# Message stage: turning a channel's factors to tokens in 64-row tiles, as products with a 64x64 identity

## The chip, the cores and the metric

The kernel runs on 1 core of one Trainium2 chip. The metric is the device time in microseconds of one execution. The times of this text are the medians of several executions.

## The reference, cut to what matters

The program is a small transformer: an attention layer, a mixture-of-experts layer, a "message" layer, and the experts layer once more, each added to x (4 batches of 1024 tokens of 128 features). The change lies in the message layer, which for each batch and each of C = 16 channels of rank R = 64 computes:

```
qz_u = qz @ ternary_factor_u.T * SCALE          # (batch, tokens, C*R)
qz_v = qz @ ternary_factor_v.T * SCALE
message_F = einsum('bcsr,bctr->bcst', qz_u, qz_v)
qh = sigmoid(message_F)
qh_v1 = einsum('bcst,bctr->bcsr', qh, qz_v)
qh_v2 = einsum('bcst,bcsr->bctr', qh, qz_u)
message_G = (qh_v1 @ ternary_factor_u + qh_v2 @ ternary_factor_v) * SCALE
```

All of it is float32.

## The kernel before

The phases follow one another: set-up, attention, experts, message, experts. `message_phase` works through 4 x 16 = 64 channels, one after the other, in a software pipeline. For one channel the factors of all 1024 tokens lie in `uv32`, a tile of 128 rows and 1024 columns: rows 0 to 63 are the sources' factors (u), rows 64 to 127 the targets' (v), the columns are tokens. `own` and `swap` hold them again, split in a high and a low part, the second with its halves of rows exchanged by DMA.

TensorE (PE) has these blocks for a channel. All of them are written out by hand in one order, in `body(b, c, n, p)`, so the order of work on PE is that of the code:

- `factors`: six products into the two PSUM banks `unit0` and `unit1`; ACT copies them to `uv32` and `own` (`empty_factors`), POOL makes the low part.
- `by_token`: `uv32` turned so that tokens are the rows. It takes eight 128x128 tiles of `uv32`, and writes four turned tiles to `unit0` and four to `unit1`. ACT copies each bank to `tok` (`empty_tokens`).
- `forces`, four times (j = 0 to 3): twelve products of 64 rows, in pairs on rows 0 to 63 and 64 to 127 of the array, into the banks `f_ps0` and `f_ps1`; ACT takes the sigmoid (`sigmoids`).
- `onto_targets`, four times: four float32 products with 64 columns of `tok` as weights.
- `onto_sources`, twice: sixteen such products with `sigT`, the sigmoid turned by DVE and shuffled by DMA.
- `message`: four float32 products of 64 rows into `unit0` and `unit1`, which DVE adds up in `msgT`.

In the loop, `by_token(n + 1)` stands between `onto_sources(n - 1, 1, ...)` and `forces(n, 3, p)`. It waits until ACT has taken the factors out of the unit banks (`uv_taken`). Behind it on PE stand `forces(n, 3)`, `onto_targets(n, 2)`, and then `message(n - 1)`, which waits until both banks were copied to `tok` (`tok_taken`), because it writes the same banks.

On ACT the order of a channel is `sigmoids` 0 and 1, `empty_factors`, `sigmoids` 2, `empty_tokens`, `sigmoids` 3.

Of the kernel before, what the change touches and what calls it, by code (L numbers as in the profile page):

```python
# [14 lines left out]
P = 128  # L15
BATCH, SEQ, DIM = 4, 1024, 128
TILES = SEQ // P
# [10 lines left out]
CH, RANK = 16, 64  # L28
# [1536 lines left out]
def message_phase(nc, k):  # L1565

    PAIRS = TILES // 2
    SIDE = TILES // 2
    MOVES = 16
    CHANNELS = BATCH * CH  # L1570
    with ExitStack() as ctx, ExitStack() as phase:
        def sb(n, shape, dt=F32):
            return ctx.enter_context(nc.sbuf_tensor(f"m_{n}", shape, dt))
# [3 lines left out]
        def sem(n):  # L1577
            sems.append(ctx.enter_context(nc.semaphore(f"m_{n}")))
            return sems[-1]

        def ps(n, width):
            return ctx.enter_context(nc.psum_tensor(f"m_{n}", [P, width], F32))
# [6 lines left out]
        uv32 = sb("uv32", [P, SEQ])  # L1589

        own, swapped_uv_st = ([sb(f"{n}{i}", [P, 2, SEQ], F32R) for i in range(2)] for n in ("own", "swap"))
        (own_hi, own_lo), (swap_hi, swap_lo) = ([[t[:, a, :] for t in both] for a in range(2)] for both in (own, swapped_uv_st))
        tok = [sb(f"tok{i}", [P, TILES, 2, RANK]) for i in range(2)]
        sig = [[sb(f"sig{i}{s}", [P, SEQ]) for s in range(2)] for i in range(2)]

        turned = [sb(f"turned{g}", [P, 4, 4, 8, STACK]) for g in range(2)]
# [6 lines left out]
        v2_ps, v1_ps = ps("v2_ps", HALF), ps("v1_ps", HALF)  # L1603
        unit = [ps(f"unit{i}", HALF) for i in range(2)]
# [3 lines left out]
        w_high, w_ready, uv_full, uv_taken, lo_ready, tok_full, tok_taken = (  # L1608
            sem(n) for n in ("w_high", "w_ready", "uv_full", "uv_taken", "lo_ready", "tok_full", "tok_taken"))
# [9 lines left out]
        def permuted(tile, h):  # L1619

            return tile.rearrange("p (s q a) -> p q s a", s=TILES, a=STACK)[:, 2 * h:2 * h + 2, :, :]

        def natural(tile):
            return tile.rearrange("p (q s a) -> p q s a", q=2, a=STACK)

        def tile_of(tile, st):
            return tile[:, st * P:(st + 1) * P]

        def channels(eng, body):

            for b in range(BATCH):
                for c in range(2):
                    body(b, c, b * CH + c, c)
                with eng.Fori(1, CH // 2 - 1) as cc:
                    for p in range(2):
                        body(b, 2 * cc + p, b * CH + 2 * cc + p, p)
                for c in (CH - 2, CH - 1):
                    body(b, c, b * CH + c, c % 2)

        def first(n):  # L1640
            return isinstance(n, int) and n == 0

        def final(n):
            return isinstance(n, int) and n == CHANNELS - 1

        def at(c, number):
            return isinstance(c, int) and c == number

        @block.sync
        def _(sp):  # L1650
            for to, of in ((slice(0, RANK), slice(RANK, P)), (slice(RANK, P), slice(0, RANK))):
                sp.dma_start(swapped_uv[to, :], k["uv"][of, :]).then_inc(factors_swapped, 16)

            def swap(m, p):

                sp.wait_ge(lo_ready, m + 1)
                dst, src = swapped_uv_st[p], own[p]
                sp.dma_start(dst[0:RANK, :, :].bitcast(F32), src[RANK:P, :, :].bitcast(F32)).then_inc(swapped[p], 16)
                sp.dma_start(dst[RANK:P, :, HALF:SEQ].bitcast(F32), src[0:RANK, :, HALF:SEQ].bitcast(F32)).then_inc(swapped[p], 16)

            def shuffle(n, g, groups):
                for i in groups:
                    for j in range(4):
                        sp.dma_start(sigT[g][j * STACK:(j + 1) * STACK, i, :, :, :],
                                     turned[g][i * STACK:(i + 1) * STACK, j, :, :, :]).then_inc(shuffled[g], 16)

            swap(0, 0)

            def body(b, c, n, p):
                sp.wait_ge(turn_ready, 8 * n + 4)  # L1670
                shuffle(n, 0, range(2))
                if not final(n):
                    swap(n + 1, 1 - p)
                shuffle(n, 0, range(2, 4))
                sp.wait_ge(turn_ready, 8 * n + 8)
                shuffle(n, 1, range(4))
            channels(sp, body)

        @block.tensor
        def _(pe):  # L1680
# [26 lines left out]
            def by_token(m):  # L1707

                pe.wait_ge(uv_taken, 2 * m + 2)
                for i in range(2):  # L1710
                    for t in range(4):
                        mm = pe.transpose(unit[i][:, t * P:(t + 1) * P], tile_of(uv32[:, :], 4 * i + t), k["ident"][:, :])  # L1712
                    mm.then_inc(tok_full, 1)

            def forces(n, j, p):

# [14 lines left out]
            def onto_targets(n, j, p):  # L1731

                if j == 0:
                    pe.wait_ge(tok_taken, 2 * n + 2)
                    if not first(n):

                        pe.wait_ge(v2_taken, n)
                pe.wait_ge(sig_ready, 8 * n + 2 * j + 2)
                for s in range(2):
                    for h in range(2):  # L1740
                        mm = pe.matmul(v2_ps[h * RANK:(h + 1) * RANK, :], tok[p][:, j + s * SIDE, 0, :],  # L1741
                                       sig[j % 2][s][:, h * HALF:(h + 1) * HALF], start=(j == 0 and s == 0), stop=(j == PAIRS - 1 and s == 1))
                mm.then_inc(p2_done, 1)

            def onto_sources(n, g, p):

                pe.wait_ge(shuffled[g], 256 * n + 256)
                if not (first(n) and g == 0):

                    pe.wait_ge(v1_taken, 2 * n + g)  # L1750
                for jj in range(TILES):
                    for h in range(2):
                        mm = pe.matmul(v1_ps[h * RANK:(h + 1) * RANK, g * 2 * P:(g + 1) * 2 * P], tok[p][:, jj, 1, :],  # L1753
                                       sigT[g][:, :, 2 * h:2 * h + 2, jj, :].rearrange("p i s a -> p s i a"), start=(jj == 0), stop=(jj == TILES - 1))
                mm.then_inc(p1_done, 1)

# [26 lines left out]
            turn_z(0)  # L1783
            factors(0, 0, 0, 0)
            by_token(0)

            def body(b, c, n, p):
# [29 lines left out]
            for g in range(2):  # L1817
                onto_sources(CHANNELS - 1, g, 1)
# [3 lines left out]
        @block.scalar  # L1822
        def _(act):
            act.wait_ge(var_ready, 1)
            act.activation(dev[:, :], spread[:, :], ACT.Sqrt).then_inc(dev_ready, 1)

            def high_z(b):
                for i in range(2):
                    act.wait_ge(z_full, 2 * b + i + 1)
                    act.copy(permuted(zT_hi[:, :], i), natural(unit[i][:, :])).then_inc(zT_high, 1)  # L1830

            def empty_factors(m, p):

                if not first(m):

                    act.wait_ge(lo_ready, m)
                for i in range(2):
                    cols = slice(i * HALF, (i + 1) * HALF)
                    act.wait_ge(uv_full, 2 * m + i + 1)
                    act.copy(uv32[:, cols], unit[i][:, :])  # L1840
                    act.copy(own_hi[p][:, cols], unit[i][:, :]).then_inc(uv_taken, 1)  # L1841

            def empty_tokens(m, p):
                for i in range(2):
                    act.wait_ge(tok_full, 2 * m + i + 1)
                    act.copy(tok[p][:, 4 * i:4 * i + 4, :, :].rearrange("p t a r -> p (t a r)"), unit[i][:, :]).then_inc(tok_taken, 1)  # L1846

            def sigmoids(n, j):

                act.wait_ge(f_full, 4 * n + j + 1)  # L1850
                if not (first(n) and j < 2):

                    act.wait_ge(p2_done, 4 * n + j - 1)
                    act.wait_ge(turn_ready, 8 * n + 2 * j - 2)
                for s in range(2):
                    act.activation(sig[j % 2][s][:, :], f_ps[s][:, :], ACT.Sigmoid).then_inc(sig_ready, 1)  # L1856

            high_z(0)
            empty_factors(0, 0)
            empty_tokens(0, 0)  # L1860

            def body(b, c, n, p):
                sigmoids(n, 0)
                sigmoids(n, 1)
                if not final(n):
                    empty_factors(n + 1, 1 - p)
                sigmoids(n, 2)
                if not final(n):
                    empty_tokens(n + 1, 1 - p)
                sigmoids(n, 3)  # L1870
                if at(c, CH - 2) and b + 1 < BATCH:
                    high_z(b + 1)
            channels(act, body)
# [200 lines left out]
```

## Time and profile before

| | |
|---|---|
| time, median of 3 executions (lowest, highest) | 3334.19 us (3330.05, 3337.33) |
| the profiled execution: time, span | 3331.9 us, 3330.1 us |
| mean granted TensorE clock | 0.937 of full speed |
| PE matmul, PE weight load, DVE, ACT, POOL busy, share of the span | 87%, 54%, 53%, 43%, 22% |

The profile is one execution of the program on the chip. PE stands for TensorE's matmuls, PEld for its weight loads, which overlap them. A matmul's duration in it is its latency through the array, and matmuls are pipelined; so what a stream of them costs is read from the distance between their starts. The granted clock is 1.00 at 2.4 GHz and 0.50 at 1.2 GHz. The message phase runs from about 1272 us to about 2912 us of the span.

### The profile page before, as it was taken

The numbers are of one execution on the slowest core, as the hardware profiler recorded it, in microseconds if no ns is written. First come the engines' busy times: TensorE is split into PE (matmuls) and PEld (weight loads), VectorE is DVE, ScalarE is ACT, GpSimd is POOL, SyncE is SP. The second block draws the span as 40 slices with busy tenths as digits, with TensorE's granted clock in tenths as the row PEclk, the third lists the DMA queues.
The fourth block names the chain that finished last, engine by engine and source line by source line (L and its number), as shares of the span: only waits on it lengthen the run. The fifth ranks groups of instructions, "written<-read, shape, count | busy, mean of one in ns | idle before, by whom it ended". The sixth has DMA issues, their size and how long they took to land. (4 is left out here: it accounts for less than half of the span.)

```text
span 3330.1 us, 55832 instructions
## 1 busy us (share of the span) xinstructions
PE 2907.6 (87%) x18642; PEld 1797.9 (54%) x18643; DVE 1755.1 (53%) x3207; ACT 1416.6 (43%) x2072; POOL 721.6 (22%) x866
## 2 busy tenths in 40 slices
PE   2888888889548996999999999999999999945897
PEld 1555554555437873555555555555555555444786
DVE  3656555554445664544554555555455555445565
ACT  1454554545424443444444444444444444332443
POOL 4131220311436330111111111111111111062632
PEclk7899999999759997999999999999999999966998
DMA  9000000000212215888888888888888888731122
GB/s 164 14 12 9 14 13 8 13 14 7 86 32 60 82 44 138 200 195 201 200 185 201 201 195 195 196 200 195 201 193 195 199 201 200 174 96 32 57 69 78
DMA packets 205987, 397.16 MB, mean 119 GB/s; under 512 B 45586, under 2 KB 118171, under 8 KB 201627
## 3 DMA queue, kind: packets, MB, share of 16 engines
q1 hardware_dynamic: 196634, 376.35, 49.1%
q0 software_dynamic: 9216, 19.02, 1.7%
q8 instruction: 82, 1.34, 0.2%
q14 instruction: 55, 0.44, 0.0%
HBM read 35.23 MB, written 31.75 MB: 20 GB/s over the span
## 5 line engine op out<-in xcount | busy, mean ns | idle before, releaser
L1943 DVE STREAM_TRANSPOSE m_turned<-m_sig 128x1024 f32<-128x1024 f32 x512 | 613.2, 1226 | 595.0 <-ACT m_sig L1856 575.3
L1856 ACT ACTIVATE m_sig<-m_f_ps 128x1024 f32<-128x1024 f32 x512 | 496.4, 1022 | 607.1 <-PE m_f_ps L1728 607.1
L1741 PE MATMUL m_v_ps<-m_sig,m_tok 128*64 128x512 f32 x2048 | 496.0, 605 | 0.0
L775 DVE TENSOR_REDUCE a_maxima<-a_pair 128x2 f32<-128x1024 f32 (+3 forms) x384 | 351.6, 953 | 272.3 <-PE a_pair L449 210.3
L1753 PE MATMUL m_v_ps<-m_sigT,m_tok 128*64 128x256 f32 x4096 | 465.5, 380 | 7.2 <-DMA m_sigT<-m_turned 7.2
L1728 PE MATMUL m_f_ps<-m_swap,m_own 64*128 64x512 f32 x1536 | 442.8, 421 | 11.0 <-DMA m_swap<-m_own 8.8
L1728 PE MATMUL m_f_ps<-m_own,m_swap 64*128 64x512 f32 x1536 | 442.9, 421 | 0.0
L593 ACT ACTIVATE a_prob<-a_pair 128x1024 f32<-128x1024 f32 (+3 forms) x384 | 303.9, 819 | 282.8 <-PE a_pair L461 282.4
L1753 PEld LDWEIGHTS m_v_ps<-m_sigT,m_tok 128*64 128x64 f32 x4096 | 293.7, 137 | 212.2 <-issue 69.5
L1728 PEld LDWEIGHTS m_f_ps<-m_swap,m_own 64*128 64x128 f32 x1536 | 270.4, 186 | 141.8 <-issue 86.2
L1880 POOL TENSOR_TENSOR m_own<-m_uv,m_own 128x1024 fp32r<-128x1024 f32 x64 | 152.0, 2375 | 840.5 <-ACT m_own L1841 840.5
L446 PE MATMUL a_pair<-k_apart,a_qT 128*128 128x512 f32 (+3 forms) x768 | 228.1, 392 | 69.6 <-DVE a_maxima L775 36.6
L1728 PEld LDWEIGHTS m_f_ps<-m_own,m_swap 64*128 64x128 f32 x1536 | 270.3, 186 | 3.4
L461 PE MATMUL a_pair<-a_qmT,k_apart 128*128 128x512 f32 (+3 forms) x768 | 238.5, 404 | 21.9 <-ACT a_prob L593 7.3
L1741 PEld LDWEIGHTS m_v_ps<-m_sig,m_tok 128*64 128x64 f32 x2048 | 124.1, 136 | 239.1 <-issue 239.1
L1329 POOL DMA_INDIRECT back_rows<-f_y_rows,f_goes_to x160 | 155.1, 970 | 263.8 <-DVE f_y_rows L1505 256.4
L446 PEld LDWEIGHTS a_pair<-k_apart,a_qT 128*128 128x128 f32 x768 | 137.6, 207 | 123.2 <-DVE a_maxima L775 62.8
L461 PEld LDWEIGHTS a_pair<-a_qmT,k_apart 128*128 128x128 f32 x768 | 122.2, 199 | 121.4 <-issue 56.9
L1175 PE MATMUL f_y_ps<-f_w_down,f_innerT 128*128 x1280 | 171.2, 277 | 6.3 <-DVE f_y_rows L1505 3.7
L1846 ACT COPY m_tok<-m_unit 128x512 f32<-128x512 f32 x128 | 68.8, 589 | 249.4 <-PE m_unit L1712 249.4
L1175 PEld LDWEIGHTS f_y_ps<-f_w_down,f_innerT 128*128 128x128 f32 x1280 | 156.3, 193 | 9.9 <-issue 9.8
L678 POOL TENSOR_TENSOR a_steps<-ones 128x1 f32<-128x1 f32 x128 | 25.5, 199 | 620.9 <-ACT a_prob L593 620.9
(284 smaller groups left out, 4006.3 us busy)
## 6 DMA issues: line engine op xcount, KB each, us to landing
m_sigT<-m_turned SPq DMA_DIRECT2D x2048, 128.0 KB, 2.4
m_swap<-m_own SPq DMA_DIRECT2D x64, 512.0 KB, 4.4
m_swap<-m_own SPq DMA_DIRECT2D x64, 256.0 KB, 5.0
f_t_rows<-f_sent_rows SPq DMA_DIRECT2D x162, 65.0 KB
f_sent_rows<-clear_rows SPq DMA_DIRECT2D x40, 260.0 KB
k_apart<-a_kT SPq DMA_DIRECT2D x64, 128.0 KB, 2.3
f_h<-back_rows SPq DMA_DIRECT2D x8, 512.0 KB, 6.4
f_norm_all<-back_rows SPq DMA_DIRECT2D x8, 512.0 KB, 5.7
```

Of the source, the lines that this page charges most:

```text
L446: mm = pe.matmul(out[:, i, :], qT[g % 2][:, qt * P:(qt + 1) * P], k_apart[g % 2][:, 2 * pair + i, k0:k1], start=True, stop=not masked)
L461: mm = pe.matmul(out[:, i, :], k_apart[g % 2][:, 2 * pair + i, j * P:(j + 1) * P], qmT[g % 2][:, q0:q1], start=True, stop=True)
L593: act.activation(prob[j % 2][:, 2 * pair:2 * pair + 2, q0:q1], src, ACT.Exp).then_inc(u.free(), 1)
L775: dve.tensor_reduce(maxima[:, qt, 2 * pair:2 * pair + 2, part], src, AX.X, ALU.max).then_inc(u.free(), 1)
L1175: mm = pe.matmul(y_ps[:, 0:DIM], innerT[p][:, ib * P:(ib + 1) * P], w_down[:, ds(e * INTER + ib * DIM, DIM)], start=(ib == 0), stop=(ib == ...
L1329: pool.indirect_dma_start(back_rows[n // HALF_NB][:, :], bass.IndirectOffsetOnAxis(ap=goes_to[n % UNROLL][:, :], axis=0), y_rows[n % RING] ...
L1728: mm = pe.matmul(f_ps[s][:, cols], tile_of(u[rows, :], j + s * SIDE), v[rows, cols], start=start, stop=stop)
L1741: mm = pe.matmul(v2_ps[h * RANK:(h + 1) * RANK, :], tok[p][:, j + s * SIDE, 0, :], sig[j % 2][s][:, h * HALF:(h + 1) * HALF], start=(j == ...
L1753: mm = pe.matmul(v1_ps[h * RANK:(h + 1) * RANK, g * 2 * P:(g + 1) * 2 * P], tok[p][:, jj, 1, :], sigT[g][:, :, 2 * h:2 * h + 2, jj, :].rea ...
L1856: act.activation(sig[j % 2][s][:, :], f_ps[s][:, :], ACT.Sigmoid).then_inc(sig_ready, 1)
L1880: pool.tensor_tensor(own_lo[p][:, :], uv32[:, :], own_hi[p][:, :].bitcast(F32), ALU.subtract).then_inc(lo_ready, 1)
L1943: dve.transpose(turned[g][:, :, q, :, :], sig[j % 2][s][:, :].rearrange("p (t j a) -> p j t a", j=4, a=STACK)).then_inc(turn_ready, 1)
```

## The change

`by_token` makes the same turned tiles in another way. Before, it issued eight 128x128 transposes (TensorE's transpose mode), each turning u and v of 128 tokens at once, so that a unit bank held [tile][u or v][64]. After, it issues sixteen ordinary float32 products (no transpose mode): for each of the eight tiles of 128 tokens, one with rows 0 to 63 as weights and the upper left 64x64 corner of the identity as the moving side, into `unit0`, and one with rows 64 to 127 and the lower right corner, into `unit1`. So `unit0` holds all sources, `unit1` all targets. The layout of `tok` follows, from [tile][u or v][64] to [u or v][tile][64], and with it the slices that `onto_targets` and `onto_sources` take as weights. The semaphore `tok_full` is still counted up once for each bank, now at the last product of each, which both stand at the end.

```diff
-        tok = [sb(f"tok{i}", [P, TILES, 2, RANK]) for i in range(2)]
+        tok = [sb(f"tok{i}", [P, 2, TILES, RANK]) for i in range(2)]
...
                 pe.wait_ge(uv_taken, 2 * m + 2)
-                for i in range(2):
-                    for t in range(4):
-                        mm = pe.transpose(unit[i][:, t * P:(t + 1) * P], tile_of(uv32[:, :], 4 * i + t), k["ident"][:, :])
-                    mm.then_inc(tok_full, 1)
+                for t in range(TILES):
+                    for a in range(2):
+                        rows = slice(a * RANK, (a + 1) * RANK)
+                        mm = pe.matmul(unit[a][:, t * RANK:(t + 1) * RANK], tile_of(uv32[rows, :], t), k["ident"][rows, rows], start=True, stop=True)
+                        if t == TILES - 1:
+                            mm.then_inc(tok_full, 1)
...
-                        mm = pe.matmul(v2_ps[h * RANK:(h + 1) * RANK, :], tok[p][:, j + s * SIDE, 0, :],
+                        mm = pe.matmul(v2_ps[h * RANK:(h + 1) * RANK, :], tok[p][:, 0, j + s * SIDE, :],
...
-                        mm = pe.matmul(v1_ps[h * RANK:(h + 1) * RANK, g * 2 * P:(g + 1) * 2 * P], tok[p][:, jj, 1, :],
+                        mm = pe.matmul(v1_ps[h * RANK:(h + 1) * RANK, g * 2 * P:(g + 1) * 2 * P], tok[p][:, 1, jj, :],
...
-                    act.copy(tok[p][:, 4 * i:4 * i + 4, :, :].rearrange("p t a r -> p (t a r)"), unit[i][:, :]).then_inc(tok_taken, 1)
+                    act.copy(tok[p][:, i, :, :].rearrange("p t r -> p (t r)"), unit[i][:, :]).then_inc(tok_taken, 1)
```

On PE the place is the middle of a channel, between the last products of `onto_sources` (L1753) and `forces(n, 3)` (L1728). Before, with each tile's buffer number (out<-moving, weights, size of the output):

```order
L1753 MATMUL m_v1_ps<-m_sigT1,m_tok1 64x256 x15
L1712 MATMUL m_unit0<-ident,m_uv32 128x128 [waits m_uv_taken]
L1712 MATMUL m_unit0<-ident,m_uv32 128x128 x3
L1712 MATMUL m_unit1<-ident,m_uv32 128x128 x4
L1728 MATMUL m_f_ps0<-m_swap0,m_own0 128x512 [waits m_sig_ready]
L1728 MATMUL m_f_ps1<-m_own0,m_swap0 128x512
```

The eight transposes fill one bank and then the other. After the change the same place begins so (two lines more in the file, so L1753 is L1755 and L1728 is L1730):

```order
L1755 MATMUL m_v1_ps<-m_sigT1,m_tok1 64x256 x15
L1713 MATMUL m_unit0<-ident,m_uv32 128x64 [waits m_uv_taken]
L1713 MATMUL m_unit1<-ident,m_uv32 128x64
L1713 MATMUL m_unit0<-ident,m_uv32 128x64
L1713 MATMUL m_unit1<-ident,m_uv32 128x64
```

and, without the buffer numbers, the same stretch to its end:

```order
L1713 MATMUL m_unit<-ident,m_uv 128x64 [waits m_uv_taken]
L1713 MATMUL m_unit<-ident,m_uv 128x64 x15
L1730 MATMUL m_f_ps<-m_swap,m_own 128x512 [waits m_sig_ready]
L1730 MATMUL m_f_ps<-m_own,m_swap 128x512
L1730 MATMUL m_f_ps<-m_swap,m_own 128x512
```

Nothing else moved: sixteen instructions stand where eight stood, they alternate between the banks (and between the two halves of the array's rows), and the waits are the same. The orders on ACT, DVE, POOL and the DMA queue are unchanged.

## Rows read from the trace of the kernel before

**Rows 1.** The page: busy time, and the granted clock in 40 slices

```profile
PE 2907.6 (87%) x18642; PEld 1797.9 (54%) x18643; DVE 1755.1 (53%) x3207; ACT 1416.6 (43%) x2072; POOL 721.6 (22%) x866
...
PEclk7899999999759997999999999999999999966998
```

**Rows 2.** Windows (us from the span's start): length, busy by engine, clock, DMA share, GB/s

```profile
1700.00:2000.00 300.00, 299.05 (x1976) 159.69 (x1973) 152.43 (x189) 130.21 (x168) 34.13 (x36) 1.00 0.86 198
2300.00:2600.00 300.00, 298.28 (x1976) 160.19 (x1976) 157.67 (x199) 130.15 (x169) 34.82 (x36) 1.00 0.86 196
```

**Rows 3.** Who PE waited for, 1300 to 2860 us: total, times, longest

```profile
PE m_f_ps L1728 <- DMA m_swap<-m_own: 2.9, 1, 2.9
PE m_unit L1712 <- DVE x L1970: 2.8, 3, 0.9
PE m_unit L1689 <- DVE m_msgT L1963: 2.3, 3, 0.8
PE m_v_ps L1753 <- DMA m_sigT<-m_turned: 0.4, 1, 0.4
```

**Rows 4.** Timeline of PE: start, us from first start to last end, instructions

```profile
1803.13 1.09 PE L1712 MATMUL m_unit<-ident,m_uv 128*128 128x128 f32 x8
1804.16 0.50 PE L1728 MATMUL m_f_ps<-m_swap,m_own 64*128 64x512 f32 x1
...
1828.19 1.09 PE L1712 MATMUL m_unit<-ident,m_uv 128*128 128x128 f32 x8
```

**Rows 5.** Groups of PE by form, with counts

```profile
L1741 PE MATMUL m_v_ps<-m_sig,m_tok 128*64 128x512 f32 x2048 | 496.0, 605 | 0.0
L1728 PE MATMUL m_f_ps<-m_own,m_swap 64*128 64x512 f32 x1536 | 442.9, 421 | 0.0
L1712 PE MATMUL m_unit<-ident,m_uv 128*128 128x128 f32 x512 | 70.9, 282 | 4.0 <-DVE x L1970 2.8 <-ACT m_own L1841 1.2
L1768 PE MATMUL m_unit<-m_v2T,m_fin_w 64*128 64x512 f32 x256 | 65.6, 589 | 0.0
L1728 PEld LDWEIGHTS m_f_ps<-m_own,m_swap 64*128 64x128 f32 x1536 | 270.3, 186 | 3.4
```

**Rows 6.** Timeline of the weight loads, by_token and forces

```profile
1803.13 0.86 PEld L1712 LDWEIGHTS m_unit<-ident,m_uv 128*128 128x128 f32 x8 [0.39 <-issue]
1804.16 0.18 PEld L1728 LDWEIGHTS m_f_ps<-m_swap,m_own 64*128 64x128 f32 x1 [0.17 <-issue]
1804.16 0.18 PEld L1728 LDWEIGHTS m_f_ps<-m_own,m_swap 64*128 64x128 f32 x1
1804.27 0.19 PEld L1728 LDWEIGHTS m_f_ps<-m_swap,m_own 64*128 64x128 f32 x1
1804.27 0.19 PEld L1728 LDWEIGHTS m_f_ps<-m_own,m_swap 64*128 64x128 f32 x1
1804.50 0.18 PEld L1728 LDWEIGHTS m_f_ps<-m_swap,m_own 64*128 64x128 f32 x1
```

**Rows 7.** Timeline of the weight loads, message and the forces behind it

```profile
1807.61 0.30 PEld L1768 LDWEIGHTS m_unit<-m_v1T,m_fin_w 64*128 64x128 f32 x4 [0.81 <-issue]
1808.14 0.19 PEld L1768 LDWEIGHTS m_unit<-m_v2T,m_fin_w 64*128 64x128 f32 x2 [0.23 <-issue]
1808.57 0.19 PEld L1768 LDWEIGHTS m_unit<-m_v2T,m_fin_w 64*128 64x128 f32 x2 [0.24 <-issue]
1809.00 0.19 PEld L1728 LDWEIGHTS m_f_ps<-m_swap,m_own 64*128 64x128 f32 x1 [0.24 <-issue]
```

**Rows 8.** Timeline of float32 products in the experts phases (L1119), weight loads

```profile
867.34 1.86 PEld L1119 LDWEIGHTS f_up<-attn_wT,f_silu 128*128 128x128 f32 x16 [0.25 <-ACT f_silu L1258]
...
3031.74 0.97 PEld L1119 LDWEIGHTS f_up<-gate_wT,f_silu 128*128 128x128 f32 x8 [0.90 <-ACT f_silu L1258]
```

**Rows 9.** The same stretches as matmuls, and their windows (clock third from the end)

```profile
867.34 2.05 PE L1119 MATMUL f_up<-attn_wT,f_silu 128*128 128x128 f32 x16
...
3031.74 1.06 PE L1119 MATMUL f_up<-gate_wT,f_silu 128*128 128x8 f32 x8 [0.50 <-ACT f_silu L1258]
...
867.30:869.40 2.10, 2.08 (x17) 1.86 (x16) 1.36 (x6) 0.78 (x1) 2.10 (x4) 1.00 0.04 10
3031.50:3032.80 1.30, 1.06 (x10) 1.06 (x10) 0.23 (x1) 0.19 (x1) 0.00 (x0) 0.96 0.00 0
```

**Rows 10.** Timeline of ACT: the two copies to tok, and the next sigmoids

```profile
1803.83 1.07 ACT L1846 COPY m_tok<-m_unit 128x512 f32<-128x512 f32 x2 [3.89 <-PE m_unit L1712]
1805.93 1.94 ACT L1856 ACTIVATE m_sig<-m_f_ps 128x1024 f32<-128x1024 f32 x2 [1.03 <-PE m_f_ps L1728]
```

## The prediction

> **What bounds the kernel now.** First the page: PE is busy 87% of the span, far ahead of every other engine, and its clock slices are lowest outside the long middle stretch [rows 1]. That stretch is the message phase, about 1640 us, half of the span. The windows inside it show PE busy 298 to 299 us of every 300 at a granted clock of 1.00, the 2.4 GHz level, while DVE and ACT are busy about half of it and the DMA engines 86% [rows 2]. Busy could still hide waits, since matmul durations are latencies, so the third view is who PE waited for: over 1560 us these waits add up to 8.4 us, and only 0.4 us of them is for the shuffled sigmoids [rows 3]. The fourth is the timeline: by_token starts at 1803.13 and again at 1828.19, a channel of 25.06 us in a window in which PE waits for nobody [rows 4]. So in this phase a channel costs what PE's own stream costs. What by_token gains or loses on PE is gained or lost 64 times, and nothing stands beside it to hide it.
>
> The part that is replaced: eight transposes from 1803.13 until the first loads and products of forces at 1804.16, which is 1.03 us [rows 4, 6]. Their weight loads begin (0.86 - 0.14) / 7 = 0.10 to 0.11 us apart [rows 6].
>
> **How many instructions come in their place.** The 512 records of L1712 are 64 channels times eight: a transpose is one record. L1741 has 64 x 4 x 4 = 1024 products in the code and 2048 records, one part of message (L1768) 64 x 2 = 128 products and 256 records [rows 5]: an ordinary float32 product is two weight loads and two matmuls. The new by_token leaves transpose mode. It issues 16 products a channel, thus 32 loads of 64x128 and 32 matmuls of 64 moving columns; PE's count should go from 18642 to 18642 + 64 x 24 = 20178.
>
> **Do the two halves run side by side?** Forces has the same form (weights 64x128, rows 0 to 63 and 64 to 127 in turn, a bank each), and its loads come in pairs with one start: two at 1804.16, two at 1804.27 [rows 6]. Message has it in plain float32 and alternates the banks product by product just as the new code does: four loads in 0.30 us, then two at 1808.14 and two at 1808.57 [rows 7]. So 32 records should be 16 pairs.
>
> **What a pair costs.** There are two bounds, the matmul and the load. The matmul: a pair of message with 512 moving columns takes 1808.57 - 1808.14 = 0.43 us [rows 7], so 64 columns take 0.43 / 8 = 0.054 us, and 16 pairs 0.86 us. The load: it has 128 columns whatever the moving side is. Where no long matmul stands in between, pairs of 64x128 loads begin 0.11 us apart: in forces 1804.16 to 1804.27 [rows 6], in message (four loads, two pairs, in 0.30 us, one load lasting 0.19) also 0.11 [rows 7]. The best row is L1119 with 8 moving columns, where the matmul is nearly nothing: eight loads in 0.97 us, (0.97 - 0.19) / 7 = 0.111 us each, at a clock of 0.96; with 128 moving columns it is (1.86 - 0.19) / 15 = 0.111 us at a clock of 1.00 [rows 8, 9]. So a float32 load of 128 columns costs 0.111 us at full clock and hides any matmul of up to 128 columns. The new block is bound by its loads: 64 rows instead of 128 make a load no cheaper (0.18 to 0.19 us of latency in forces), and 64 moving columns instead of 128 save nothing.
>
> I take 0.110 us a pair; the rows allow 0.108 to 0.112.
>
> The Trainium skill speaks for the change here: the page "TensorEngine Tiling (Array Packing)", section "Theoretical Speedup", gives up to twofold for a contraction of 64 rows or less. Applied to the matmuls alone that is the 0.86 us above. The page "TensorE: Matmul & The Clock Gate", section "LDWEIGHTS (loading the stationary operand)", speaks against it: a load's time goes by its columns and not by its rows, which is what the load rows show.
>
> **The seam to forces.** The last transpose load starts about 0.14 us before 1803.99 (1803.13 + 0.86), at 1803.85, and the loads of forces begin 0.31 us behind it, three times the spacing inside the block; then a load of 0.11 us must pass before forces can stream [rows 6]. Message, whose weights have the shape of those of forces, has no such gap: the first load of forces at 1809.00 follows the last one of message by the 0.43 us of its stream [rows 7]. The new by_token has that shape too. So the gap of about 0.2 us goes; it lies inside the 1.03 us that I compare with, and the new block is counted with no gap. The seam ahead of it stays as it is, since onto_sources (128x64) changes the shape before either.
>
> The same skill page on tiling says, in "Key Properties", that a change of tiling mode drains the engine; the gap of 0.2 us in front of forces agrees. By that rule alone, with all else free, the change would gain 0.2 us a channel.
>
> **The sum.** New block, first load to the loads of forces: 16 x 0.110 = 1.76 us. Before: 1.03 us. A channel grows by 0.73 us, to 25.79 us. For 64 channels that is +46.7 us; 0.108 gives 0.70 and +44.7, 0.112 gives 0.76 and +48.8. Against the profiled execution's own 3331.9 us (1.8 us around the span) this is 3378.6; the median of the three runs is 2.3 us higher, so 3381. I say 3380.
>
> **What costs nothing.** (1) ACT's copies: before, the first began at 1803.83, halfway through the transposes, and both took 1.07 us. Now both banks fill at the end, so they begin about 0.2 us after the last product, near 1803.13 + 1.76 + 0.2 = 1805.1, and end at 1806.2. The next sigmoid would start at 1805.93 + 0.73 = 1806.66 [rows 10], and is not delayed. If it were, forces(n + 1, 0) would wait, which comes behind onto_targets and message, some 3.3 us later. Message waits for the same copies, and stands behind forces and onto_targets, also over 3 us away. (2) The new layout of tok: the same 64 contiguous columns are loaded, and ACT copies the same 128x512. (3) Swap, shuffle and DVE gain 0.73 us of slack a channel. As PE waits for them 0.4 us in 1560 us [rows 3], that gives back nothing.
>
> **The rivals.**
> - Faster, load half as long. If a load of 64 rows cost half (0.055 us), the matmul bound of 0.054 us would meet it: 16 x 0.055 = 0.88 us against 1.03, -0.15 us a channel, -9.6 us, 3324 us. It decides for faster once a pair costs less than 1.03 / 16 = 0.064 us. For it: the design gives each half its own rows and bank. Against it: two places where 64-row pairs follow each other 0.11 us apart. Chance 5%. The skill's twofold, above, is this case.
> - Slower still, load and matmul in line. If a short matmul isn't hidden behind the next load, a pair costs 0.110 + 0.054 = 0.164: 2.62 us, +1.59 a channel, +102 us, 3436 us. For it: eight transposes come 0.11 us apart though loads in transpose mode are shorter (0.14 against 0.19), so something there is in line. Against it: L1119 with 128 columns costs no more than with 8. Chance 6%.
> - No pairs. 32 x 0.110 = 3.52 us, +2.49 a channel, +159 us, 3493 us. Only forces and message speak on that, both with long matmuls, and both pair. Chance 4%.
> - No change (within 0.2%, or 7 us, about what a measurement of this kernel can tell): the 0.73 us would have to vanish in waits that PE has at present, which are at most 8.4 us in all. Chance 2%.
> - The forecast, +44 to +49 us: 83%, in which I count small surprises at the seams of 0.15 us a channel either way.
>
> **Numbers.** The forecast's 0.15 us of seam is 10 us, so 3369 to 3392; I stretch the upper end a little toward the case in line: 3368 to 3398. Faster 0.05, same 0.02, slower 0.93.
>
> **What would show it.** In the new profile: L1713 with 2048 matmuls and as many loads; its loads in pairs, 0.11 us apart, about 1.76 us from the first to the first load of forces, which follows without the 0.3 us gap; a channel of 25.8 us; PE still without waits; the time outside the message phase unchanged. I am wrong if pairs follow each other in under 0.064 us, if the halves come singly, or if PE begins to wait for the sigmoids or the copies.

## The result, and the profile after

The changed kernel takes 3383.14 us (median of 4, 3379.43 to 3385.09), the kernel before 3333.36 us beside it (median of 4). The ratio is 1.0147, its 95% interval 1.0132 to 1.0163: slower by 49.8 us. The prediction was 3380 us in a range of 3368 to 3398, at a chance of 0.93 for slower.

The page of the kernel after, busy time and clock slices (they answer to [rows 1]):

```profile
span 3377.7 us, 58904 instructions
PE 2955.4 (87%) x20178; PEld 1858.3 (55%) x20179; DVE 1755.0 (52%) x3207; ACT 1416.5 (42%) x2072; POOL 721.5 (21%) x866
...
PEclk7899999999669988999999999999999999966998
```

PE's count is 20178, the number forecast; DVE, ACT and POOL have their old counts and busy times. Who PE waited for, 1300 to 2900 us of the kernel after, beside [rows 3]:

```profile
PE m_f_ps L1730 <- DMA m_swap<-m_own: 2.9, 1, 2.9
PE m_unit L1713 <- DVE x L1972: 2.8, 3, 0.9
PE m_unit L1689 <- DVE m_msgT L1965: 2.3, 3, 0.8
PE m_v_ps L1755 <- DMA m_sigT<-m_turned: 1.0, 1, 1.0
```

The same waits as before, 9.0 us in all against 8.4. Nothing absorbed the change, and no new wait came. The timeline of PE in the kernel after (start, us, instructions), beside [rows 4]:

```profile
1844.48 2.00 PE L1713 MATMUL m_unit<-ident,m_uv 64*128 64x64 f32 x32
...
1870.31 0.89 PE L1713 MATMUL m_unit<-ident,m_uv 64*128 64x64 f32 x12
```

A channel now takes 1870.31 - 1844.48 = 25.83 us where it took 25.06. The medians over all 64 channels are the same two numbers. 0.77 us times 64 is 49.3 us, so the difference lies here. The weight loads of the same stretch, beside [rows 6]:

```profile
1844.48 1.86 PEld L1713 LDWEIGHTS m_unit<-ident,m_uv 64*128 64x128 f32 x32 [0.39 <-issue]
1846.26 0.19 PEld L1730 LDWEIGHTS m_f_ps<-m_swap,m_own 64*128 64x128 f32 x1
1846.27 0.19 PEld L1730 LDWEIGHTS m_f_ps<-m_own,m_swap 64*128 64x128 f32 x1
1846.37 0.19 PEld L1730 LDWEIGHTS m_f_ps<-m_swap,m_own 64*128 64x128 f32 x1
```

There are 32 loads in 1.86 us, and the last lasts 0.19: 15 steps of 0.111 us if they come in pairs. The loads of forces begin 1.78 us after the first of the block (1.03 before). The gap ahead of forces is gone: from the last pair at 1844.48 + 1.86 - 0.19 = 1846.15 to forces at 1846.26 is one more step of 0.11.

ACT, beside [rows 10]:

```profile
1846.51 1.07 ACT L1848 COPY m_tok<-m_unit 128x512 f32<-128x512 f32 x2 [5.22 <-PE m_unit L1713]
1848.05 1.02 ACT L1858 ACTIVATE m_sig<-m_f_ps 128x1024 f32<-128x1024 f32 x1 [0.46 <-PE m_f_ps L1730]
```

The copies begin only after the block, as expected, and still leave ACT idle for 0.46 us before the next sigmoids (1.03 before). They delay nothing.

### The profile page after: what moved, and what is told of

It is laid out like the page before. It is cut to its first block and busy times, and to the rows that moved or that the text cites. A ratio compares the mean times of both kernels' runs of the same rounds, so it can differ in the third digit from the quotient of the medians.

```text
span 3377.7 us, 58904 instructions
## 1 busy us (share of the span) xinstructions
PE 2955.4 (87%) x20178; PEld 1858.3 (55%) x20179; DVE 1755.0 (52%) x3207; ACT 1416.5 (42%) x2072; POOL 721.5 (21%) x866
## 5 line engine op out<-in xcount | busy, mean ns | idle before, releaser
L1755 PE MATMUL m_v_ps<-m_sigT,m_tok 128*64 128x256 f32 x4096 | 465.8, 380 | 7.5 <-DMA m_sigT<-m_turned 7.5
L1730 PE MATMUL m_f_ps<-m_swap,m_own 64*128 64x512 f32 x1536 | 441.1, 419 | 9.2 <-DMA m_swap<-m_own 7.0
L1730 PE MATMUL m_f_ps<-m_own,m_swap 64*128 64x512 f32 x1536 | 440.7, 419 | 0.0
L1755 PEld LDWEIGHTS m_v_ps<-m_sigT,m_tok 128*64 128x64 f32 x4096 | 294.4, 137 | 211.7 <-issue 73.7
L1730 PEld LDWEIGHTS m_f_ps<-m_swap,m_own 64*128 64x128 f32 x1536 | 269.7, 185 | 131.2 <-issue 75.5
L1730 PEld LDWEIGHTS m_f_ps<-m_own,m_swap 64*128 64x128 f32 x1536 | 269.7, 185 | 0.8
L1888 POOL COPY m_fin_w<-uv 128x128 f32 (+1 forms) x64 | 18.6, 290 | 672.5 <-PE m_unit L1770 672.5
```

The source lines that it names most:

```text
L1730: mm = pe.matmul(f_ps[s][:, cols], tile_of(u[rows, :], j + s * SIDE), v[rows, cols], start=start, stop=stop)
```

## The experiments

The theory: the block costs what its float32 weight loads cost, two a product, 0.111 us for 128 columns, whatever the rows and whatever the moving columns up to 128. The rivals: 64-row tiles are slow by themselves; load and matmul are in line; the matmul sets the pace; the new layout of `tok` costs something where it is read. e1, e2, e4 and e6 were timed beside one another, with the kernel before at 3331.52 us (15 runs).

**e1: 64-row tiles, in transpose mode.** The tiles, banks and layout of the change, with the first tile as products and the others as transposes:

```diff
-                        mm = pe.matmul(unit[a][:, t * RANK:(t + 1) * RANK], tile_of(uv32[rows, :], t), k["ident"][rows, rows], start=True, stop=True)
+                        product = unit[a][:, t * RANK:(t + 1) * RANK], tile_of(uv32[rows, :], t), k["ident"][rows, rows]
+                        mm = pe.matmul(*product, start=True, stop=True) if t == 0 else pe.transpose(*product)
```

> The tiles, banks and layout of the changed kernel, but in transpose mode for seven of the eight tiles (one record each, 14 transposes of 64x128), the first tile as two ordinary products. Theory (the block costs what its float32 loads cost, two a product): two pairs of 0.111 us and seven pairs of transposes. If a transposed pair costs the 0.109 us of the old transposes, the block is 0.99 us against 1.03 us before and 1.78 us after, the time 3330 to 3334 us; if its shorter load (0.14 against 0.19 us of latency) sets the pace at 0.055 us, the block is 0.61 us and the time about 3306 us. Rival (64-row tiles themselves, not the leaving of transpose mode, made it slow): the time stays near 3383 us.

Measured: 3308.60 us (5 runs), ratio to before 0.9934 (0.9920 to 0.9947). Loads, and PE's timeline over a channel:

```profile
1824.46 0.74 PEld L1714 LDWEIGHTS m_unit<-ident,m_uv 64*128 64x128 f32 x18 [0.39 <-issue]
1825.11 0.20 PEld L1731 LDWEIGHTS m_f_ps<-m_swap,m_own 64*128 64x128 f32 x1
```

```profile
1824.46 0.88 PE L1714 MATMUL m_unit<-ident,m_uv 64*128 64x64 f32 x18
...
1849.18 0.50 PE L1714 MATMUL m_unit<-ident,m_uv 64*128 64x64 f32 x6
```

A transpose is one load and one matmul, so there are 4 + 14 = 18 records instead of 32. The loads of forces begin 0.65 us after the first of the block (1.03 before, 1.78 after). Take off two pairs at 0.111, and seven pairs of transposes take 0.43 us, 0.061 each. The channel is 24.72 us; 0.34 us less than before, times 64, is 21.8 us, and 22.9 were measured. The block of 0.65 us is near the second of the two cases (0.61 us). So 64-row tiles are not slow: what made the change slow is that it left transpose mode. With transposes the same tiling beats both kernels. The number of records is one part of it: a pair of transposes is one step, a pair of products two. The length of a step is the other: 0.061 us against 0.111, though the loads have 128 columns in both. So 0.111 us belongs to the loads of ordinary float32 products and not to 128 columns as such.

**e2: twice the moving columns.** 14 of the 16 products move 128 columns of the identity instead of 64. Their surplus columns fall on those of a neighbouring tile, which is written afterwards; for that the targets' tiles go backwards:

```diff
-                        mm = pe.matmul(unit[a][:, t * RANK:(t + 1) * RANK], tile_of(uv32[rows, :], t), k["ident"][rows, rows], start=True, stop=True)
+                        at_t, cols = (t, slice(0, RANK)) if a == 0 else (TILES - 1 - t, rows)
+                        wide = slice(at_t * RANK, (at_t + 1) * RANK)
+                        if t < TILES - 1:
+                            cols = slice(0, P)
+                            wide = slice((at_t - a) * RANK, (at_t - a + 2) * RANK)
+                        mm = pe.matmul(unit[a][:, wide], tile_of(uv32[rows, :], at_t), k["ident"][rows, cols], start=True, stop=True)
```

> The changed kernel with 128 moving columns instead of 64 in 14 of the 16 products (the surplus columns are overwritten by the next product). Theory (the load of 128 columns sets the pace and hides a matmul of up to 128 columns): pairs still 0.111 us apart, the same time, 3383 us within 2 us. Rival, load and matmul in line: 14 of 16 pairs grow by 0.054 us, +0.75 us a channel, +48 us, 3431 us. Rival, the matmul alone sets the pace: the pairs would double, +99 us.

Measured: 3379.76 us (4 runs), ratio to before 1.0148 (1.0132 to 1.0163), where the change has 1.0147. Its loads and its matmuls:

```profile
1839.31 1.86 PEld L1718 LDWEIGHTS m_unit<-ident,m_uv 64*128 64x128 f32 x32 [0.39 <-issue]
1841.09 0.19 PEld L1735 LDWEIGHTS m_f_ps<-m_swap,m_own 64*128 64x128 f32 x1
```

```profile
1839.31 2.00 PE L1718 MATMUL m_unit<-ident,m_uv 64*128 64x128 f32 x32
```

The 32 loads again take 1.86 us, and forces again begins 1.78 us in. The median lies 3 us under the change's, just outside the 2 us, but the ratio, the block and the channel (25.83 us) are those of the change. Doubling the matmuls' work cost nothing. The rivals "in line" (3431 us) and "the matmul alone" (+99 us) fall.

**e3: half the columns in a load.** Seven tiles as products of 64 rows by 64 columns of weights, four to a tile:

```diff
-                        mm = pe.matmul(unit[a][:, t * RANK:(t + 1) * RANK], tile_of(uv32[rows, :], t), k["ident"][rows, rows], start=True, stop=True)
+                        if t == 0:
+                            mm = pe.matmul(unit[a][:, t * RANK:(t + 1) * RANK], tile_of(uv32[rows, :], t), k["ident"][rows, rows], start=True, stop=True)
+                            continue
+                        for h in range(2):
+                            half = slice(h * RANK, (h + 1) * RANK)
+                            mm = pe.matmul(unit[a][half, t * RANK:(t + 1) * RANK], tile_of(uv32[rows, :], t)[:, half], k["ident"][rows, rows], start=True, stop=True)
```

> Seven of the eight tiles as ordinary float32 products of 64 rows by 64 columns of weights, four to a tile of 128 tokens, so that every load has 64 columns instead of 128; the first tile as in the changed kernel. Theory (a pair costs the columns of its load): 2 pairs at 0.111 us, then 14 sets of four loads at 0.055 us, and a gap of 0.2 to 0.3 us at the change of shape ahead of forces: 1.25 to 1.35 us against 1.78, about 3351 us. Rival 1 (only two of the four run side by side): 28 x 0.055 instead, block about 2.1 us, about 3400 us. Rival 2 (each product has a floor of its own, whatever the columns): no faster than 3383 us.

Measured: 3279.21 us (4 runs). It ran with e8 on a chip where the kernel before takes 3256.76 us, so only the ratio can be set beside the others: 1.0070 (1.0051 to 1.0090), between before and the change (1.0147). Of 3333 us that is +23 us, where 3351 meant +18; the interval, +17 to +30, holds both. Its loads:

```profile
1800.96 0.30 PEld L1714 LDWEIGHTS m_unit<-ident,m_uv 64*128 64x128 f32 x4 [0.39 <-issue]
1801.33 0.91 PEld L1718 LDWEIGHTS m_unit<-ident,m_uv 64*64 64x64 f32 x56
1802.30 0.18 PEld L1735 LDWEIGHTS m_f_ps<-m_swap,m_own 64*128 64x128 f32 x1
```

56 loads in 0.91 us, each 0.135 long: 13 steps of 0.060 us if they go four at a time, about half the step of 128 columns. The block is 1802.30 - 1800.96 = 1.34 us, in the forecast 1.25 to 1.35. The rest of it are the two changes of shape: 0.26 us from the last 64x128 load (1801.07) to the first 64x64 one, and 0.20 us from the last of those (1802.10) to forces. All of its arithmetic is that of the change; only the products are cut in half, so that they load 64 columns and run four at a time. That rules out a floor of 0.111 us for every product. It doesn't show that the load still sets the pace: the prediction's other bound, 0.054 us for a matmul of 64 moving columns, lies as near to 0.060.

**e4: one half, then the other.**

```diff
-                for t in range(TILES):
-                    for a in range(2):
+                for a in range(2):
+                    for t in range(TILES):
```

> The changed kernel with its two loops exchanged: all eight products of rows 0 to 63 first, then all eight of rows 64 to 127. Theory (a load runs beside another only when neighbours in the order use different rows): 32 loads one by one at 0.111 us, 3.56 us instead of 1.78, +114 us, 3497 us. Rival (loads are pulled ahead across the order, or the pairing isn't what halves the cost): 3383 us or little above.

Measured: 3471.17 us (2 runs), ratio 1.0418 (1.0399 to 1.0437): 1.40 us a channel over the change (27.23 against 25.83), where 1.78 were expected. The loads at the end of the block, and PE's timeline there and one channel later:

```profile
1877.13 2.92 PEld L1713 LDWEIGHTS m_unit<-ident,m_uv 64*128 64x128 f32 x29 [0.39 <-issue]
1879.92 0.18 PEld L1730 LDWEIGHTS m_f_ps<-m_swap,m_own 64*128 64x128 f32 x1
1879.97 0.19 PEld L1713 LDWEIGHTS m_unit<-ident,m_uv 64*128 64x128 f32 x1
1880.03 0.18 PEld L1730 LDWEIGHTS m_f_ps<-m_swap,m_own 64*128 64x128 f32 x1
1880.08 0.30 PEld L1713 LDWEIGHTS m_unit<-ident,m_uv 64*128 64x128 f32 x2
```

```profile
1877.13 3.06 PE L1713 MATMUL m_unit<-ident,m_uv 64*128 64x64 f32 x29
1879.92 0.50 PE L1730 MATMUL m_f_ps<-m_swap,m_own 64*128 64x512 f32 x1
1880.03 0.49 PE L1713 MATMUL m_unit<-ident,m_uv 64*128 64x64 f32 x3
...
1904.36 0.32 PE L1713 MATMUL m_unit<-ident,m_uv 64*128 64x64 f32 x1
```

The direction is that of the theory, and the size was off by a fifth. The theory said "only neighbours". In fact forces, whose first product uses rows 0 to 63, begins while rows 64 to 127 still work through their last three by_token records. 29 loads take (2.92 - 0.19) / 28 = 0.098 us each and not 0.111, so some overlap inside the block too. The trace's single records show where: within a half the loads follow each other by 0.112 us, and the first load of the second half begins at 1878.53, before the last three of the first half (the last of them at 1878.80). Three steps saved are 0.33 of the 0.38 us that the theory had too much. So the halves run beside each other over a distance of a few records, not only as neighbours.

**e6: the layout alone.** The old transposes on PE (`by_token` as it was before), with ACT's copies writing the new layout:

```diff
...
-                    act.copy(tok[p][:, i, :, :].rearrange("p t r -> p (t r)"), unit[i][:, :]).then_inc(tok_taken, 1)
+                    act.copy(tok[p][:, :, 4 * i:4 * i + 4, :].rearrange("p a t r -> p t a r"), unit[i][:, :].rearrange("p (t a r) -> p t a r", t=4, a=2)).then_inc(tok_taken, 1)
```

> The old transposes on PE, and the new layout of tok, made by ACT's copies, which read and write in 64-column pieces. Theory (the layout of tok costs nothing where it is read): the time of the kernel before, 3333 us within 4 us, and ACT's copies near 0.587 us each. Rival (part of the 50 us comes from the weights' new place in tok): up to 3383 us, with onto_targets or onto_sources slower.

Measured: 3331.08 us (10 runs), ratio 1.0001 (0.9992 to 1.0011). The group of ACT's copies:

```profile
L1846 ACT COPY m_tok<-m_unit 128x512 f32<-128x512 f32 x128 | 68.9, 590 | 248.7 <-PE m_unit L1712 248.7
```

590 ns each, against 589 before. The layout of `tok` costs nothing, neither in the copies nor where it is read.

**e8: one product only.** e1 with `if t == a == 0` in place of `if t == 0`.

> As e1, but only one product of a channel (sources, first tile) stays an ordinary one, the other fifteen are transposes of 64x128. Theory (a load of an ordinary product 0.111 us, a pair of transposes 0.062 us as e1 measured): one lone load goes from the block. 3308.6 us of e1, less at most 0.05 us a channel: 3305 to 3309 us, ratio to before 0.992 to 0.9935. Rival (each switch between product and transpose costs a drain, and more of them stand here): above 3309 us.

Measured: 3240.89 us (6 runs), ratio 0.9948 (0.9930 to 0.9967) beside its own 3256.76 us. That is faster than before. It lies above the 0.992 to 0.9935 that was expected, though the interval reaches into it, and the interval overlaps that of e1, so their order is not settled by the times. The traces tell more (PE's timeline, with ACT's copies in their place):

```profile
1794.45 0.74 PE L1714 MATMUL m_unit<-ident,m_uv 64*128 64x64 f32 x15
1794.99 0.47 PE L1731 MATMUL m_f_ps<-m_own,m_swap 64*128 64x512 f32 x1
1795.03 0.29 PE L1714 MATMUL m_unit<-ident,m_uv 64*128 64x64 f32 x2
...
1795.35 1.07 ACT L1849 COPY m_tok<-m_unit 128x512 f32<-128x512 f32 x2 [4.10 <-PE m_unit L1714]
...
1819.14 0.47 PE L1714 MATMUL m_unit<-ident,m_uv 64*128 64x64 f32 x6
```

A channel is 24.69 us against 24.72 in e1 (medians of all channels 24.70 and 24.72), so one product less is worth 0.02 to 0.03 us a channel, at most 2 us in all. The rival of a drain at each switch isn't really tested by it: in the order of the code e8 goes from product to transpose once in a channel, as e1 does, and not more often. What speaks against such a drain is e1's block, in which the seven pairs of transposes take 0.43 us with the switch into them, and no gap stands out.

Both halves into one bank wasn't tried, so what a bank for each half is worth is not shown.

## Why the prediction was right

- **PE's stream sets the channel.** Right. The channel time times 64 gives +49.3 us (change), -21.8 (e1), each within about 1.1 us of the measured difference; PE's waits stayed at about 9 us. Outside the phase little changed: it begins at 1273.9 where it began at 1272.6, and from the start of the last by_token to the end of the span it is 465.5 us where it was 465.9.
- **Two records a product, PE at 20178.** Right, to the record.
- **Halves side by side.** Right: e4, without the alternation, costs 1.40 us a channel more.
- **0.110 us a pair, set by the load.** The measured step is 0.111. e2 shows that the matmul has no share in it up to 128 moving columns. e3 shows that it is no fixed cost of a product: with half the columns of weights the step is 0.060. This was the one decisive step, and it rested on L1119 [rows 8, 9], a line of another phase whose moving side is 8 columns wide. The rule quoted from the Trainium skill's page "TensorE: Matmul & The Clock Gate", section "LDWEIGHTS (loading the stationary operand)", that columns and not rows count, agrees as far as ordinary products go: 64 rows saved nothing, 64 columns went with about half the step. The transposes of e1, 0.061 us a step with 128 columns, don't fit one cost for a number of columns. The twofold gain that the Trainium skill's page "TensorEngine Tiling (Array Packing)", section "Theoretical Speedup", gives as the most was not had here: the block grew from 1.03 to 1.78 us.
- **The seam.** Right: the gap of 0.31 us between last load and forces fell to one step of 0.11. In e1, with transposes of that same shape, it is gone as well, and in e3, with another shape, 0.20 us stand there where a step inside its block is 0.06. So it belongs to the change of shape and not to transpose mode.
- **The sum.** 0.73 us was forecast, 0.77 measured: 0.75 to the start of forces (1.78 against 1.03), and 0.02 that have come in by the end of the forces directly behind it. The two halves enter them 0.01 us apart (1846.26 and 1846.27, where both stood at 1804.16 before); that this is the cause is not shown. Times 64 the error is 2.6 us of 49.8.
- **What costs nothing.** Right: the copies left 0.46 us of idle time ahead of the sigmoids, and e6 clears the layout.

Not settled: what sets the 0.061 us of a pair of 64x128 transposes, against 0.11 for one of 128x128 by itself and 0.111 for a pair of ordinary loads. Between the two kinds of transposes both the moving columns and the concurrency differ, and no run separates the two.

## What to carry to other kernels

Before cutting float32 products into smaller tiles, count weight loads: an ordinary float32 product loads its weights twice, 0.111 us each for 128 columns whatever the rows, and a matmul of up to 128 moving columns hides behind that. A transpose written as a product with the identity therefore does twice the loads of a transpose, and in 64-row tiles each step was longer as well (a pair 0.22 against 0.061 us). If tiling by rows is wanted, keep transpose mode, which here, for 14 of the 16, turned +1.5% into -0.7%. Neighbouring blocks of one tile shape saved 0.14 to 0.20 us at their seam.

## What the runs showed that was not expected

In e4 matmuls started out of program order: one of forces at 1879.92, ahead of the last three of by_token, from 1880.03, which stand before it and use the other half of the rows. e8 shows it too: a product of forces on rows 64 to 127 starts at 1794.99, ahead of the last two of by_token on rows 0 to 63, from 1795.03. It is so in 63 of the 64 channels of both runs. The Trainium skill's page "TensorE: Matmul & The Clock Gate", section "The mechanism", says that matmuls start and end in program order; the starts in these traces do not.

Of the semaphores the same can't be said. In e8 the half that is ahead, rows 64 to 127, has the last product of the code, and it ends 0.13 us before the last one of rows 0 to 63. Had `tok_full` been counted up at that end (about 1795.18), ACT's copies, which wait for the first count, could have begun at about 1795.22. They begin at 1795.35, 0.03 us after the end of the half that lags (1795.03 + 0.29 = 1795.32). In the times that the trace gives for the count itself, the first of a channel comes 0.014 us after that end, in all 64 channels. So no count is seen to overtake work that stands ahead of it in the code, though the starts do; the ends are modelled, so this is the likely reading and no proof.

And e3 ran four loads and four matmuls in a step of 0.060 us, so issue did not bind at 8 instructions in 60 ns.
